# Loads in two queues, another order between the layers and four banks for the last scores, in a two-layer kernel

## What is computed

```python
xn = layernorm(x)
x = x + linear_attention(xn) + moe(xn)       # layer 1
xn = layernorm(x)
x = x + chunked_attention(xn) + gated_ffn(xn)   # layer 2
```

## Time and profile before

| | us |
|---|---|
| median of 3 runs | 1524.6 (1523.17 to 1528.86) |
| profiled execution | 1515.43 |
| its span | 1513.5 |
| start and body 0, up to body 1's first cut | 0 to 73 |
| bodies 1 to 15 | 73 to 511 |
| experts | 511 to 796 |
| layer 2 and tail | 796 to 1513.5 |
| TensorE busy | 1404.1 |
| VectorE busy | 1177.3 |
| ScalarE busy | 817.2 |
| GpSimd busy | 523.3 |

### The profile page before, as it was taken

One profiled execution on the slowest core, in us unless ns is written; L12 is line 12 of the kernel. 1 busy time (PEld: TensorE's weight loads), 2 busy tenths in 40 slices (PEclk: granted clock), 3 DMA queues, 4 the chain that ended last, 5 costly groups with the idle time before them and its releaser, 6 DMA issues.

```text
span 1513.5 us, 35393 instructions
## 1 busy us (share of the span) xinstructions
PE 1404.1 (93%) x12926; PEld 904.6 (60%) x12926; DVE 1177.3 (78%) x2687; ACT 817.2 (54%) x1562; POOL 523.3 (35%) x942
## 2 busy tenths in 40 slices
PE   5699999999999899999998999999999999999994
PEld 3467677677776799998884444444444444444432
DVE  4789889889888795456677888888888888888752
ACT  2334534544543333334334677777766777776673
POOL 2333234234233111172312244444434444442121
PEclk8999999999999999999999999999999999999997
DMA  4111111111112566776973444333334443332300
GB/s 119 38 42 52 45 48 44 51 47 44 54 33 66 165 208 209 220 245 208 258 195 62 98 106 105 98 98 102 87 93 102 108 103 97 98 92 70 82 9 14
DMA packets 118205, 151.94 MB, mean 100 GB/s; under 512 B 31269, under 2 KB 83109, under 8 KB 113413
## 3 DMA queue, kind: packets, MB, share of 16 engines
q1 hardware_dynamic: 105160, 119.47, 29.0%
q0 software_dynamic: 12880, 30.30, 6.8%
HBM read 108.35 MB, written 40.83 MB: 99 GB/s over the span
## 4 chain that ended last, share of the span: by engine, by line
PE 48%; DVE 32%; POOL 7%; issue 6%; ACT 5%; DMA 1%; SPq 0%; POOLq 0%; DVEq 0%; ACTq 0%
DVE nmax L1516 8%; PE bank L1948 8%; PE bank L1939 8%; DVE P L1205 7%; PE bank L1816 5%; PE bank L1994 5%; PE bank L2017 4%; ACT P L946 3%; PE bank L1773 3%; PE bank L1850 2%; PE bank L1957 2%; PE bank L1864 2%; DVE t L1080 1%; PE bank L2064 1%; DVE t L1078 1%
## 5 line engine op out<-in xcount | busy, mean ns | idle before, releaser
L1516 DVE TENSOR_REDUCE nmax<-bank 128x1 f32<-128x512 f32 (+3 forms) x704 | 428.8, 634 | 84.6 <-PE bank L1994 83.6
L946 ACT ACTIVATE P<-bank 128x512 f32<-128x512 f32 x640 | 371.2, 599 | 183.2 <-PE bank L2017 178.4
L1994 PE MATMUL bank<-KT,QT 76*128 76x512 bf16 (+3 forms) x1024 | 251.3, 303 | 28.5 <-DVE nmax L1516 20.9
L2017 PE MATMUL bank<-QT,KT 78*128 78x512 bf16 (+3 forms) x1024 | 244.5, 301 | 8.9 <-ACT P L946 5.5
L693 POOL DMA_INDIRECT xs_d<-xn,idx x128 | 124.6, 973 | 306.0 <-PE bank L1773 197.9
L1994 PEld LDWEIGHTS bank<-KT,QT 76*128 76x128 bf16 x1024 | 86.8, 97 | 189.1 <-DVE nmax L1516 130.6
L1816 PE MATMUL bank<-P,V 128*32 128x512 f32 (+3 forms) x2048 | 191.3, 447 | 0.0
L1205 DVE TENSOR_TENSOR P<-bank,early_w 128x512 f32<-128x512 f32 x256 | 158.7, 682 | 41.3 <-PE bank L1773 41.2
L910 ACT ACTIVATE hr<-bank 128x512 f32<-128x512 f32 x142 | 84.8, 597 | 175.0 <-PE bank L1939 172.1
L741 POOL DMA_INDIRECT hT<-ys_d,idx x104 | 103.5, 995 | 159.9 <-PE bank L2017 141.8
L2017 PEld LDWEIGHTS bank<-QT,KT 78*128 78x128 bf16 x1024 | 98.6, 98 | 85.0 <-ACT P L946 31.9
(11 more groups left out here) (257 smaller groups left out, 2228.6 us busy)
## 6 DMA issues: line engine op xcount, KB each, us to landing
QT<-parts_d SPq DMA_DIRECT2D x96, 192.0 KB
P<-in_fc SPq DMA_DIRECT2D x71, 256.0 KB, 2.9
P<-in_proj SPq DMA_DIRECT2D x71, 256.0 KB, 3.2
parts_d<-parts SPq DMA_DIRECT2D x32, 384.0 KB, 2.5
P<-xs_d SPq DMA_DIRECT2D x71, 128.0 KB, 3.0
ys_d<-P POOLq DMA_DIRECT2D x71, 128.0 KB, 3.4
KT<-parts_d SPq DMA_DIRECT2D x64, 128.0 KB
KT<-parts_d SPq DMA_DIRECT2D x32, 192.0 KB
```

Source lines behind the costliest of these rows:

```text
L946: nc.scalar.activation(P[s % 2][:, u, :], bank[k % 2][:, :], ACT.Exp, scale=float(DH) ** -0.5).then_inc(s_sb, 1)
L1516: nc.vector.tensor_reduce(nmax[:, s // TWO, h:h + TWO * nh - 1:TWO, j], max_bank(n, k)[:, 0:nh * w].rearrange("p (h w) -> p h w", h=nh), A ...
L1994: ins = pe.matmul(max_bank(n, k)[:, i * w:(i + 1) * w], QT[n.p][0:MROWS, h, j * 128:(j + 1) * 128], KT[n.p][0:MROWS, h, 0:w], start=True, ...
L2017: ins = pe.matmul(bank[k % 2][:, c:c + n], KT[b.p][0:SROWS, h, 128 * kb:128 * kb + 128], QT[b.p][0:SROWS, h, 128 * kb:T], start=True, stop ...
```

## The change

Start: half of the table `rope` is issued by GpSimd; `rope_loaded` becomes two semaphores. The four constants that the first cut and the ranks need (`tri`, `ebase`, `lower`, `before`) get a semaphore of their own and are loaded first; the wait for the other 13 moves to TensorE's first `shared_fc` and VectorE's body 1. TensorE does scores 1 of batch 0 ahead of body 0, VectorE its router right after the first cut. In body 0 GpSimd does the root first and all eight scatters after it, and VectorE does cut 1 first and `ln(2)` behind the second `y_out`. Last body of layer 1: `residual(14)` goes ahead of `row_terms` and `expert_terms`; three of four `shared_fc` and their squares go earlier. Last pass of scores: from unit 4 on four banks in turn.

```diff
+        def score_bank(b, k):
+            return bank[k % 4 if b.known() == L2 + B - 1 and k >= LAG else k % 2]
+        def load_rope(eng, g, a):
+            rows = slice(QUAD * g + QUAD // PAIRS * a, QUAD * g + QUAD // PAIRS * (a + 1))
+            eng.dma_start(rope[rows, :, :], io["rope"].rearrange("(d a g b) k t -> g a b d (k t)", a=PAIRS, g=G, b=TWO)[g, a]).then_inc(rope_loaded[a], 16)
 # SP
-            for g, a in itertools.product(range(G), range(PAIRS)): (rope, all eight)
+            for g in range(G):
+                load_rope(sp, g, 0)
             load_x(Turn(0, 1))
...
+            for t, src in masks:
+                sp.dma_start(t[tuple(slice(None) for _ in t.shape)], src).then_inc(masks_loaded, 16)
 # GpSimd
             def body(b, first, last):
+                if first:
+                    ln_root(b + 2)
+                    scatter(b, range(2 * J))
+                    return
...
+            for g in range(G):
+                load_rope(pool, g, 1)
             pool.wait_ge(ln_consts, 3)
             ln_root(Turn(0, 0))
 # ScalarE
+                if last:
+                    for k in range(NB - 1):
+                        square_h(b, k)
                 evac_oT(b, 1)
-                for k in range(NB):
+                for k in range(NB - 1 if last else 0, NB):
                     square_h(b, k)
...
-                nc.scalar.activation(P[s % 2][:, u, :], bank[k % 2][:, :], ACT.Exp, ...)
+                nc.scalar.activation(P[s % 2][:, u, :], score_bank(b, k)[:, :], ACT.Exp, ...)
 # VectorE, body
+                if first:
+                    cut(b, 1)
+                elif b.known() == 1:
+                    dve.wait_ge(consts_loaded, 16 * CONSTS)
...
-                cut(b, 1)
+                if not first:
+                    cut(b, 1)
                 if first:
-                    router(b)
                     router_pick(b)
...
-                if last:
-                    row_terms(0)
-                    expert_terms()
                 if not last:
                     feature(b + 1)
                 if not first:
                     residual(b + -1)
                 if last:
+                    row_terms(0)
+                    expert_terms()
                     first_tiles()
...
-                if more:
+                if more and not first:
                     ln(b + 2)
...
                 y_out(b, 1)
+                if first:
+                    ln(b + 2)
 # VectorE, start
-            dve.wait_ge(consts_loaded, 16 * CONSTS)
+            dve.wait_ge(masks_loaded, 16 * MASKS)
             nc.vector.tensor_copy(fill[:, :], ebase[:, 0, :]).then_inc(zeroed, 1)
             cut(first, 0)
+            router(first)
 # TensorE
             def shared_fc(b, k, last):
+                if early(b, 1) and k == 0:
+                    pe.wait_ge(consts_loaded, 16 * CONSTS)
...
-                scores(b, 1)
+                if not first:
+                    scores(b, 1)
...
                 attend_narrow(b, 1)
+                if last:
+                    shared_fc(b, 0, last)
+                    shared_fc(b, 1, last)
...
+                if last:
+                    shared_fc(b, 2, last)
                 turn_oT(b, 0)
...
             sum_states(n0)
-            pe.wait_ge(consts_loaded, 16 * CONSTS)
+            scores(n0, 1)
 # TensorE, shifted_scores
-                if not (b.less(L2 + 1) and k < 2):
+                four = b.known() == L2 + B - 1 and k >= LAG
+                if four and k >= 2 * LAG:
+                    pe.wait_ge(s_sb, b.at(PASS, k - 3 - PASS * L2))
+                elif four and k % 4 >= 2:
+                    pe.wait_ge(max_read, b.at(MAXES, MAXES - MAXES * L2))
+                elif not (b.less(L2 + 1) and k < 2):
                     pe.wait_ge(s_sb, b.at(PASS, k - 1 - PASS * L2))
```

More of the change, by code:

```diff
@@ L46 @@
 DEN_EPS = 1e-6
-CONSTS = 17
+CONSTS, MASKS = 13, 4
 TAU = 12.5
@@ L245, in build @@
         consts_loaded, zeroed, ready_consts = sem("consts_loaded"), sem("zeroed"), sem("ready_consts")
-        wqk_loaded, wvr_loaded, ident_loaded, rope_loaded, own_loaded = (
-            sem(s) for s in ("wqk_loaded", "wvr_loaded", "ident_loaded", "rope_loaded", "own_loaded"))
+        masks_loaded = sem("masks_loaded")
+        wqk_loaded, wvr_loaded, ident_loaded, own_loaded = (
+            sem(s) for s in ("wqk_loaded", "wvr_loaded", "ident_loaded", "own_loaded"))
+        rope_loaded = [sem(f"rope_loaded{a}") for a in range(PAIRS)]
         ln_consts = sem("ln_consts")
@@ L437, in _ @@
         def _(sp):
-            loads = [(lower, io["lower"]), (before, io["before"]), (ebase, io["ebase"]), (tri, io["tri"]),
-                     (wo, io["wo"]), (sfc, io["fc"][E]), (spj, io["proj"][E]),
+            masks = [(tri, io["tri"]), (ebase, io["ebase"]), (lower, io["lower"]), (before, io["before"])]
+            loads = [(wo, io["wo"]), (sfc, io["fc"][E]), (spj, io["proj"][E]),
                      (incl, io["incl"]), (tiles, io["tiles"]), (steps, io["steps"]),
@@ L450, in _ @@
             sp.dma_start(ident[:, :], io["ident"]).then_inc(ident_loaded, 16)
-            for g, a in itertools.product(range(G), range(PAIRS)):
-                rows = slice(QUAD * g + QUAD // PAIRS * a, QUAD * g + QUAD // PAIRS * (a + 1))
-                sp.dma_start(rope[rows, :, :], io["rope"].rearrange("(d a g b) k t -> g a b d (k t)", a=PAIRS, g=G, b=TWO)[g, a]).then_inc(rope_loaded, 16)
+            for g in range(G):
+                load_rope(sp, g, 0)
             load_x(Turn(0, 1))
@@ L945, in exp_scores @@
                 act.wait_ge(s_ps, b.at(PASS, k + 1 - PASS * L2))
-                nc.scalar.activation(P[s % 2][:, u, :], bank[k % 2][:, :], ACT.Exp, scale=float(DH) ** -0.5).then_inc(s_sb, 1)
+                nc.scalar.activation(P[s % 2][:, u, :], score_bank(b, k)[:, :], ACT.Exp, scale=float(DH) ** -0.5).then_inc(s_sb, 1)
             def square_k(n):
@@ L1449, in _ @@
             first = Turn(0, 0)
-            dve.wait_ge(rope_loaded, 16 * G * PAIRS)
+            for a in range(PAIRS):
+                dve.wait_ge(rope_loaded[a], 16 * G)
             rotate(first, 0)
@@ L1730, in prefix @@
             def prefix(n):
+                if early(n, 1):
+                    pe.wait_ge(masks_loaded, 16 * MASKS)
                 pe.wait_ge(picked, n.at(1, 1))
@@ L1906, in body @@
                         turn_y(b)
-                    shared_fc(b, k, last)
+                    if not last or k == 3:
+                        shared_fc(b, k, last)
             pe.wait_ge(rows_ordered, 4 * PAIRS)
@@ L2016, in shifted_scores @@
                     n = T - 128 * kb
-                    ins = pe.matmul(bank[k % 2][:, c:c + n], KT[b.p][0:SROWS, h, 128 * kb:128 * kb + 128],
+                    ins = pe.matmul(score_bank(b, k)[:, c:c + n], KT[b.p][0:SROWS, h, 128 * kb:128 * kb + 128],
                                     QT[b.p][0:SROWS, h, 128 * kb:T], start=True, stop=True)
```

## The result

The kernel after the change took 1517.0 us at the median (1509.4 to 1520.5, 9 runs) against 1524.7 before it (1523.2 to 1531.8, 9 runs): ratio 0.9933, 95% interval 0.9907 to 0.9959. The two medians lie 7.7 us apart; the ratio is worth 10.2 us, with 6.3 to 14.2 for its interval. 12.0 were forecast. So it is faster by 0.67% (0.41 to 0.93), and the median of 1517.0 is inside the range forecast. Run again unchanged in two later sets, on a chip where the kernel before took 1516.7 and 1517.4, it gave 0.9913 [0.9884, 0.9941] and 0.9908 [0.9891, 0.9925], which is 13.2 and 14.0 us.

What follows compares the result with a forecast made beforehand. Unedited bodies keep TensorE busy 28.10 of 29.00 us, so gains lie only where order breaks: first batch, layer one's last body, last score pass; 8.5 - 0.7 + 4.2 = 12.0 us, median 1512.6, range 1507.5 to 1519.5.

Steps and rivals of the forecast that it cites:

- rival 3: Start gives only half, as GpSimd's scatters in a row or a constant behind the masks hold VectorE; 1516.9, chance 0.1.
- its own sign: Forecast wrong if body 1 starts within 5 us of before, or the last pass is under 2 us shorter.
- Table, -0.1: First rotation: table on two queues gains 0.1 us, GpSimd's issues lose 0.2; bounds -1.9 and +0.1.
- Rival 4: Start: GpSimd's half of the table lands one DMA after another, far too late; slower, 1529, chance 0.05.
- Masks, 3.3, high bound 4.8: First batch: masks and second sheet's scores sooner gain 3.3 us; low 2.3, high 4.8 if 2.4 GHz comes sooner.
- Scatters, 5.3: First batch: VectorE's 5.63 us stall on scatters goes, 5.3 us gained net; low 3.5, high 5.8.
- Sum of the start 8.5: Start, first batch: table, masks and scatters together, -0.1 + 3.3 + 5.3 = 8.5 us gained.
- Between the layers, -0.7: Last body of layer one: reorder loses 0.7 us, as half clock outweighs an earlier yT copy; from +0.6 to -2.3.
- Banks, 4.2: Last pass of scores: four banks bring the gate 1.7 us earlier and gain 4.2 us; bounds 1.7 and 5.5.
- the two prices that I gave (5.5 and 4.0): Last pass, four banks: 5.5 us gained at full clock, 4.0 with half clock after TensorE's gap.
- Rival 1: Last pass: ScalarE's longer wait at tanh_resp eats the four banks' gain, leaving 1.7 us; 1515.1, chance 0.2.
- Rival 2: Clock: both gaps, between the layers and in the last pass, are followed by 1.2 GHz; 1514.4, chance 0.2.

Runs made afterwards that it cites:

- b3: The changed kernel with the whole rotation table issued by SP as in the kernel before; ratio 0.9943 to the kernel before.
- b4: The changed kernel with 84 more waits on TensorE's queue ahead of its first matmul, shifting its code some 5 KB; ratio 0.9955 to the kernel before.
- d1: The changed kernel, unchanged, run again in the third set; median 1504.0 us, ratio 0.9908 to the kernel before.
- d0: The kernel before, unchanged, run and profiled in the third set; median 1517.4 us.
- a1: The changed kernel, unchanged, run again in the first set; ratio 0.9913 to the kernel before.
- d2: The kernel before with only table, masks, router and scores 1 as changed; ratio 0.9974, 3.9 us faster.
- a2: The changed kernel with the order between the layers and the two banks of before, so the start alone; ratio 0.9925 to the kernel before, 11.4 us.
- b2: The kernel before with only batch 0's root first, eight scatters in a row and the normalisation of batch 2 behind y_out; ratio 0.9974, 4.0 us faster.
- b1: The kernel before with only the work between the layers reordered (shared projections 0 to 2, three squares, residual sooner); ratio 0.9997.
- d3: The changed kernel with batch 30's small steps between gate and response on VectorE, not GpSimd; median 1498.8 us, ratio 0.9870 to the kernel before.
- a3: The kernel before with only the four banks in the last pass; ratio 0.9973, 4.1 us faster.

## Why the prediction was right, and where it was off

**The verdict and its cause.** Faster, for the reasons given. The first comparison by itself (10.2 us, 6.3 to 14.2) doesn't tell 12.0 from less. Beside the other sets a loss shows that lies in no term of the sum. In the first profile the last cut of batch 0 loses 3.18 + 0.72 = 3.9 us, in b3 3.23 and in b4 2.99; by their ratios these kernels gave 10.2, 8.7 and 6.9 us. On the chip without the stall the changed kernel gave 13.2 and 14.0. So 12.0 lies between two kinds of run that the prediction didn't know of; that part is luck. That the median, 1517.0, falls on rival 3's 1516.9 is chance too. Rival 3's path isn't there: `ln(2)` doesn't wait for the scatters (62.14 has no wait), and no constant holds VectorE. But it named the scatters in a row, and they may be behind the stall by way of TensorE's marks (last section). The margin against its own sign was small in the first profile, where body 1 starts 5.6 us sooner and 5 was the limit.

**Table, -0.1.** Right. GpSimd issued its four in 2.45 us, at 0.61 each where I took 1.02, and the root started at 5.12 (5.23 before). The sine product started at 16.50; 16.6 was forecast. b3 and b4 put the two queues at some tenths of a us, with the table still ahead of the second matmul's end. Rival 4 is dead.

**Masks, 3.3, high bound 4.8.** The points forecast are met to 0.3: first cut 27.49 (27.8), second 34.26 (34.5). Then the ranks come at 38.96 without a wait, where 40.9 was forecast and 44.23 measured in the profile of before: 5.3, beyond the high bound of 4.8. The reason given with that bound, the clock, fits: the granted clock in 31 to 35 and in 35 to 38.5, in the kernel before, in d1, and in d0:

```profile
31.00:35.00 4.00, 3.14 (x14) 2.82 (x14) 2.36 (x10) 0.00 (x0) 0.00 (x0) 0.50 0.04 11
35.00:38.50 3.50, 3.50 (x52) 2.89 (x54) 0.71 (x2) 0.59 (x1) 0.00 (x0) 0.50 0.00 0
```
```profile
31.00:35.00 4.00, 4.00 (x42) 3.50 (x42) 3.01 (x7) 0.00 (x0) 0.00 (x0) 0.54 0.02 4
35.00:38.50 3.50, 3.50 (x44) 2.19 (x43) 3.43 (x16) 0.59 (x1) 0.20 (x1) 1.00 0.01 2
```
```profile
31.00:35.00 4.00, 3.23 (x74) 2.93 (x74) 2.61 (x11) 0.59 (x1) 0.00 (x0) 1.00 0.03 7
35.00:38.50 3.50, 2.15 (x14) 0.68 (x4) 3.33 (x9) 0.00 (x0) 0.00 (x0) 1.00 0.00 0
```

But the last pair is of the kernel before as well, with 2.4 GHz from 31: its ranks come at 40.68, and in d1 at 39.21, so that beside it the part is worth 1.5. All profiles together tell more. With the masks as before the level came back between 36.7 and 38.6 in five and at 30.7 in d0; with the masks ahead, between 31.0 and 35.2 in all eight (in a1 by the matmuls' durations, as its first record of the clock is at 32.7). The ranks come at 43.2 in the mean of the six and at 38.7 in the mean of the eight, 4.5 sooner, inside the bounds and above the 3.3 taken. The term that was set too low is the clock's; d2's time gives 3.9.

**Scatters, 5.3.** Right where TensorE's marks are in time. With the masks ahead in all, d2's body 1 starts at 68.67 and a2's, d1's and a1's at 63.11, 62.82 and 62.35: 5.6 to 6.3. Where the marks are late the stall takes part of it back (b2's body 1 starts 4.3 sooner than b1's, in the same order of the masks). The parts that I priced came as priced: 0.91 of idleness for the router (0.9), 1.90 at the next first cut (1.75). Sum of the start 8.5; profiles of a1, a2 and d1 give 10.7, 10.0 and 10.3 against that of before, and d1 against d0 7.8.

**Between the layers, -0.7.** Not settled by the time: b1 has 0.5 us [-1.5, +2.4]. In the rows two steps failed. First, at full clock the last cut, and y behind it, come no later: it starts 12.81 us after body 15's first in d0 (488.88 - 476.07) and in d1 (481.04 - 468.23). In b1, where those projections ran at half clock, it is 13.79 against 13.13 in b2, near the 0.6 forecast. Second, I let the copy of yT gain 0.5, and it gained 1.6: the turn of y comes 0.4 sooner, and the copy follows it 0.7 us after its start and not 1.9, as no square of ScalarE stands between. In d0 and then d1, TensorE (turn of y, `project_out`, for d1 also the rows of tile 4, counted from 0):

```profile
500.85 0.60 PE L1839 MATMUL bank<-ident,y 128*128 128x128 f32 x4
...
503.32 1.16 PE L1864 MATMUL bank<-early_w,hT 128*128 128x128 f32 x8 [1.65 <-ACT yT L850]
```
```profile
492.59 0.66 PE L1869 MATMUL bank<-ident,y 128*128 128x128 f32 x4 [1.26 <-DVE y L1241]
...
493.92 1.16 PE L1896 MATMUL bank<-early_w,hT 128*128 128x128 f32 x8 [0.46 <-ACT yT L868]
...
510.34 0.44 PE L1966 MATMUL bank<-ident,P 128*128 128x128 f32 x2 [1.05 <-DMA P<-xs_d]
```

`project_out` comes 27.25 after body 15's first cut in d0 and 25.69 in d1. Of these 1.56 us 1.2 are lost at the last row, 1.05 of them its wait: tile 4 waits for its rows, which no edit made earlier. By tile 5 the gain is 0.3. I had looked for the next wait before the experts only. The half clock forecast is there in the first profile after (0.50 in 505.5 to 512, `project_out`'s eight matmuls 2.08 instead of 1.16), in d3 (0.54 in 491 to 498.4) and, ending before `project_out`, in b3 (0.50 in 505 to 508.4); it is absent in a1, d1, b1 and b4. None of the seven profiles with the order of before has it at the turn of y. Six of them have it earlier, as d0 (0.95 in the whole window): `project_out` comes at 27.24 in a2, which has none, and between 27.25 (d0) and 28.33 (a3) in these. Where it covers `project_out`, tile 5 comes 0.7 us later than in d0 (46.92 after body 15's first cut in the first profile after, 46.19 in d0), as the -0.7 had it. Over all profiles tile 5 starts at 46.4 in the seven with the new order (45.9 to 47.1) and at 46.5 in the seven with that of before (46.2 to 47.3): the part is worth about nothing. The rule of the Trainium skill that I leaned on ("TensorE: Matmul & The Clock Gate", Part 1) agrees with the profiles that have it, and the others show that the emptier order alone doesn't decide it.

**Banks, 4.2.** Right, with its rivals in it. The gate moved 2.0 nearer the pass's start in all profiles (17.73 to 15.74; 1.7 forecast), and GpSimd is waited for 2.80 to 2.83 (2.5). From the pass's first exponential to the last values' end the gain against the profile of before is 4.15 in the first profile after, 5.64 in a1 and 1.41 in d1: the two prices that I gave (5.5 and 4.0), and one below them and below the 2 us that I had named as a sign of being wrong. But that compares profiles with different clocks. The seven profiles with two banks take 37.9 (five) and 39.4 (b2, d0), the six with four banks 32.2 (a1), 33.7 (after), 34.7 (a3, b3), 36.5 (d1) and 36.6 (b4): 3.6 less on average. Paired by the time at half clock behind the wait, it is 4.2 (37.9 and 33.7) and 4.7 (39.4 and 34.7). What separates a1 from d1 is only the clock behind the same wait. TensorE in a1, then in d1:

```profile
1471.14 0.39 PE L2061 MATMUL bank<-QT,KT 78*128 78x512 bf16 x1 [2.69 <-ACT P L967]
...
1476.75 2.36 PE L1846 MATMUL bank<-P,V 128*32 128x512 f32 x32
```
```profile
1468.99 0.61 PE L2061 MATMUL bank<-QT,KT 78*128 78x512 bf16 x1 [2.69 <-ACT P L967]
...
1478.83 2.36 PE L1846 MATMUL bank<-P,V 128*32 128x512 f32 x32
```

5.61 us and 9.84 for the same work, at a granted clock of 1.00 and of 0.61 in the windows from 1468 to 1479 and from 1466 to 1479. I had priced half clock behind the gap at 1.5; it costs up to 4.2. Rival 1, which has 1.7, is refuted by the pairs of equal clock. Rival 2 comes true in part: in the last pass the clock fell behind the wait in five of six profiles with four banks, and in all seven with two; at both places it did so in the first profile after and in b3.

## What to carry to other kernels

Compare the stages that a change doesn't touch before those that it does: one execution's 9.7 us in unedited bodies had turned a gain into a loss in the pair of profiles, and a profile 9 us under its own median was the first sign of it. Follow a gain past the next engine to the next load, here the rows of tile 4. Where an engine waits for a chain of small dependent steps on GpSimd while VectorE stands idle, move the chain: at 5.3 us it was worth nearly as much as the largest part of this change. Where TensorE's clock falls at different moments from one execution to the next, compare profiles with the same clock in the stage, or the means of several: one pair gave 1.4 for the banks, and all together 3.6.

## What the hardware did that I had not expected

- **Late marks.** In all five profiles with bodies of 29.74 to 29.8, TensorE's semaphore marks of the fourth sheet's scores come 1.3 us late in bodies 1 to 13 (1.5 to 1.6 us behind the start of the last matmul, not 0.23), at unchanged starts of the matmuls around them; in the nine others they come in time in every body. The kernel before differs by 11.4 us between the two chips. Moving the 16 KB loads of instructions by 3 to 4 us changed nothing. The cause is open.
- **The stall in batch 0.** With marks late and eight scatters in a row (first profile after, b2, b3, b4), VectorE lost 2.2 to 3.9 us at the last cut and TensorE had "issue" gaps up to 1.1 us while they were issued; b1, with late marks but scatters in two groups of four, waited 0.1. b1 and b2 differ in the first batch by the scatters, the root and the late normalisation alone, and their marks are 0.7 and 2.1 us late there; the four profiles with such a row on the other chip (a1, a2, d1, d3) have them in time. That points at the row of scatters together with what makes marks late, but it is one profile of each, and a start with the sooner masks and split scatters was not run on that chip, so it stays argued.
- **The clock.** In the kernel before it returned to 1.00 at 38.6, 36.7 and 30.7 us in three profiles, and behind one and the same 2.69 us wait it fell in d1 and not in a1. For an execution this is worth 3.6 us in the ranks (44.23 and 40.68) and 4.2 in the last pass.
- **Direct DMAs on GpSimd** were issued at 0.61 us each when four of them stood in a row for 16 rows of the table, below the 0.72 that one keeps it in the experts.
